# Eight slots for the exponentials, four products in one PSUM bank, and a key mask moved from TensorE to VectorE

## The chip, the core and the metric

One core of one Trainium2 chip runs the whole program. The metric is the device time of one execution in microseconds (us); a verdict compares medians of several runs. TensorE is called PE here, VectorE DVE, ScalarE ACT, GpSimd POOL, and SP is the engine that issues the DMAs.

## What is computed

The input x is 32 batches of 256 tokens with 256 features. Two attention blocks follow each other. Cut to what matters:

```python
# layer 0: linear attention, 8 heads of 32, softmax of k over the tokens
k = xn @ Wk + bk + (1.0 - src_mask) * -1000000.0
q = softmax(q.reshape(b, t, h, dh), axis=-1); k = softmax(k.reshape(b, t, h, dh), axis=1)
att = einsum('bnhd,bnhl->bhdl', k, v);  y = einsum('bnhd,bhdl->bnhl', q, att)
x = x + silu(_ln(y) * (1 + scale) + shift) @ W_out + b_out
# layer 1: full attention, 16 heads of 16, 256 x 256 scores
att = softmax(einsum('bnhl,bmhl->bnmh', q, k) + mask, axis=2)
y = einsum('bnmh,bmhl->bnhl', att, v)
x = x + silu(layer_norm(y) * (1 + scale) + shift) @ out_w + out_b
```

All masks of the inputs are ones; the kernel still applies them. Everything is float32.

## The kernel before

The work of a batch is cut into pieces, small functions that each run on one engine and end with an increment of a semaphore that bears the piece's name. PE has 18 kinds of piece for each batch, DVE, ACT and POOL have theirs. For each engine the pieces of all 32 batches stand in one hand-kept order (the long lists such as `rows(9, 0); rows(9, 1); pv(7, 0); ...` at the end of each engine's function), so that layer 0 of a batch runs beside layer 1 of an earlier one. An engine never goes round a piece that waits. Two tables at the top say which PSUM bank a piece writes (`BANK`) and which pieces must have ended before it may (`FREED`, waited for by `clear`, line 468). There are eight banks of 512 float32 per partition.

The pieces that the change and the prediction touch:

- `k0(b)` (PE, line 722): keys of layer 0, feature-major, 12 matmuls of 256 columns (line 733; weights and activations are each split into two f16 parts, three products), and after each half one more matmul (line 735) with a stationary operand `augs` of six rows that hold the bias in three bf16 parts and ones, against `augm`, whose rows 3 to 5 hold the mask in three bf16 parts. `am(b)` (SP, line 534) loads those rows, 1.5 KB a batch.
- `km(b)` (DVE, line 1215) takes the maximum over the tokens out of the PSUM bank of k0, `kn` (POOL) turns it into a bias, and `ke(b)` (ACT, line 1671) reads the same bank, takes the exponential with the scale in register `r_un`, and sums it. Then come `ktT` (transposes, line 718), `kt`, `att` (line 771) and `y0` (line 784).
- `rows(b, u)` and `cols(b, u)` (PE, lines 832 and 845), eight each a batch: the scores of layer 1, once for the maximum and once for the exponential. `max_` (DVE, line 1301) takes the maxima of rows, 128x1024 each. `exp(b, u)` (ACT, line 1783) writes 128x1024 exponentials of cols into one of five slots `PX`, chosen by `(8 * b + u) % 5`; it waits until `pv` of five units before has ended.
- `pv(b, u)` (PE, line 858): four matmuls of 256 columns in float32 (each stands twice in the trace), exponentials times values. The pairs u = 0,1 to 6,7 each write 256 columns of a bank of their own. `yt(b, g)` (ACT, line 1791), four a batch, copies each 128x256 to `YT`, and `ty` (PE, line 870) transposes that.
- Set-up: `row3` (PE, line 961) makes the bias of the keys as three equal rows with line 965 and 967; `p3` (DVE, line 1481) splits it into bf16 parts, `pa` (ACT) scales, `mb0` (DVE, line 1472) splits the mask in three, and the loads `mbd0`, `am` follow. `bb0`, `bb1`, `bb2` make three other biases (lines 976, 978), `fx0` (line 1002) the conditioning of layer 0.

In the written order of PE, `pv` and `att` stand in 140 unbroken stretches between pieces of other kinds, and pieces that use the full array (`k0`, `q0`, `v0`, `q1p`, `k1p`, `v1p`, `o0`, `o1`) are followed by another kind 177 times.

Of the kernel before, what the change touches and what calls it, by code (L numbers as in the profile page):

```python
# [13 lines left out]
P = 128  # L14
# [74 lines left out]
    "gy1T": "40666042444266640062604440660666",
    "go1": "23552057726271557471227354230111",  # L90
# [5 lines left out]
    "gpm": "-",  # L96
    "gt_w0": "hot",
    "ga_w0": "mx_w0",
    "gcnd": "-",
    "gbb1": "-",  # L100
    "grow3": "-",
    "gt_o0": "w0p",
    "gbb0": "-",
    "gfx0": "csT",
    "gq0": (
        "mx_o0 q1:1 mx_f0 perm qt:3 kt:5 Y0:5 at:7 qa:5 max:31 yt:11 yt:16 exp:41 exp:48 yt:28 yt:32 yt:35 Y0:16 "
        "max:102 at:19 st1:12 yt:54 yt:60 yt:64 st1:16 yt:71 yt:75 yt:79 Y0:27 max:190 exp:185 v:32 "),
    "gfm0": "mc",
    "gk0": (
        "fy0 bc0 at:2 mx_w1 bm Y0:4 max:2 exp:1 max:21 yt:8 yt:10 at:11 yt:19 yt:24 st1:6 vt:11 max:83 q1:18 Y0:17 "  # L110
        "yt:48 at:20 at:21 exp:120 yt:61 at:24 Y0:24 at:26 max:174 Y0:27 at:29 at:30 at:31 "),
    "gv0": (
        "bc1 p3 st0:1 w1p qt:3 kt:5 at:6 film1 exp:9 max:29 at:10 st0:9 yt:20 q1:14 x1:12 st1:7 st1:8 exp:84 Y0:17 "
        "max:110 st1:12 ka:18 st0:20 max:141 st1:16 st0:23 exp:153 max:174 yt:84 yt:88 exp:185 exp:191 "),
    "gt_f0": "f0m",
    "gkt": (
        "- qt:1 v:3+x1:1 bc2+at:3 v:4+ke:5 at:5+mx_f1 qt:6 yt:3+yt:2 max:25 q1:10+max:31 exp:26 exp:36 exp:45 qt:13 "
        "Y1:7 exp:68 max:91 qt:17 max:104 qt:19 exp:107 Y1:14 exp:125 exp:131 exp:137 exp:150 max:170 max:178 Y1:21 "
        "qt:29 Y1:23 exp:196 "),
    "gqt": (  # L120
        "kt:1 Y0:1 st0:2 Y0:3 qt:4 max:7 max:15 max:23 max:32 exp:27 Y1:4 max:57 Y1:6 max:72 exp:69 exp:73 Y1:10 "
        "exp:94 max:111 kt:21 max:128 Y1:15 max:144 exp:138 v:26+st0:23 exp:155 at:27+q1:28 exp:173 Y1:22 exp:187 "
        "st0:29 st1:24 "),
    "gat": (
        "q1:2 o0p kt:3 qa:1 vt:1 max:2 q1:7 kt:8 max:28 max:38 yt:15 yt:17 x1:10 Y0:13 max:75 exp:72 max:95 max:98 "
        "max:108 max:116 st1:13 st0:20 max:141 max:148 Y0:24 kt:26 yt:78 yt:83 yt:87 max:196 exp:191 Y0:31 "),
    "ga_o0": "ke:2",
    "gy0": (
        "ke:1+v:1 kt:2 kt:4 st0:3 kt:6 max:10 exp:7 max:27 max:36 exp:31 max:50 qt:12 max:68 max:74 max:84 exp:79 "
        "max:100 exp:95 max:115 exp:110 exp:119 max:138 exp:134 max:157 exp:149 exp:158 max:181 qt:28 exp:182 qt:30 "  # L130
        "max:211 max:218 "),
    "ga_f0": "v:2",
    "grw": "at:1",
    "gt_w1": "q1:3",
    "gy0T": (
        "qt:2 Y0:2 v:5+ka:1 max:3 Y0:6 Y0:7 yt:7+at:9 exp:24 exp:32 max:53 at:13+yt:23 yt:27+yt:26 max:76 max:85 "
        "exp:80 exp:87 Y0:18 max:117 Y0:20 Y0:21 st1:15 max:150 max:156 max:165 exp:160 exp:169 max:188 st1:22 "
        "max:203 max:213 max:220 max:229 "),
    "ga_w1": "film0",
    "gcol": "ke:3",  # L140
    "go0": (
        "st0:1 ke:4 qt:5 ke:7 q1:8 v:9 vt:5 ka:7 o:3 qa:9 v:14 exp:59 v:16 ka:13 ke:18 o:10 o:11 o:12 ke:22 ka:19 "
        "o:15 o:16 vt:21 o:18 yt:80 kt:29 exp:179 yt:93 exp:195 o:24 o:25 o:26 "),
    "gt_b": "q1:4",
    "ga_b": "mx_b",
    "gbb2": "kt:3",
    "gq1": (
        "fcs v:6 max:8 vt:3 exp:9 x1:7 o:2 ka:8 ke:13 x1:11 exp:59 x1:13 vt:12 exp:84 exp:90 exp:98 ka:17 x1:19 "
        "at:22 ka:20 ka:21 ka:22 exp:153 x1:25 ke:29 x1:27 o:22 ka:28 ka:29 vt:29 ka:31 o:27 "),
    "gfx1": "x1:2",  # L150
    "gk1": (
        "q1:5 q1:6 vt:2 ke:8 x1:6 o:1 v:11 v:12 v:13 o:5 qa:11 o:7 o:8 vt:13 max:102 v:20 v:21 o:13 v:23 vt:19 q1:25 "
        "ke:26 ke:27 o:19 q1:29 exp:179 q1:31 exp:195 yt:100 qa:30 vt:30 vt:31 "),
    "gfm1": "fy1",
    "gv1": (
        "at:4 Y0:5 ka:3 max:21 v:10 yt:12 max:46 max:56 st0:11 st1:6 exp:63 q1:17 yt:40 yt:45 max:110 yt:52 yt:55 "
        "qa:19 at:23 yt:68 o:17 yt:76 ka:24 max:183 max:190 yt:92 ke:32 at:32 st1:25 yt:107 max:237 yt:115 "),
    "gt_f1": "f1m",
    "gt_o1": "Y0:4",
    "gr0": (  # L160
        "ke:6+mx_o1 x1:4+v:7 exp:4 exp:11 exp:19 Y1:3 exp:35 vt:8+max:56 exp:53 kt:15 max:80 Y1:9 max:96 exp:91 "
        "max:112 exp:108 kt:22 exp:123 exp:132 max:152 exp:147 v:27+qa:23 exp:161 exp:171 o:21+q1:30 max:200 "
        "vt:27+o:23 exp:202 exp:212 exp:219 exp:227 exp:234 "),
    "gr1": (
        "x1:3+qt:5 o1p+qa:3 exp:6 qt:8 exp:21 max:41 exp:37 exp:44 kt:14 qt:14 kt:16 exp:76 exp:85 kt:19 exp:100 "
        "exp:109 exp:117 max:137 max:145 max:153 max:160 qt:26 max:177 max:185 kt:30 exp:188 max:209 exp:203 max:224 "
        "max:233 exp:228 exp:236 "),
    "gr2": (
        "max:1 max:9 v:8+ka:4 kt:9 max:33 max:42 max:49 kt:13 exp:52 exp:61 qt:15 max:90 kt:18 exp:93 max:114 qt:20 "
        "exp:118 exp:126 qt:23 exp:140 exp:148 max:169 Y1:20 max:186 exp:181 Y0:30 kt:32 exp:206 exp:214 exp:221 "  # L170
        "max:242 max:249 "),
    "gr3": (
        "ka:2+qa:2 kt:7 max:17 exp:13 max:35 yt:13+qa:7 exp:39 max:59 exp:54 yt:29+yt:30 max:82 exp:77 yt:41+qa:14 "
        "max:107 exp:101 max:123 qa:18+yt:57 Y0:22 max:146 exp:142 max:163 max:171 max:179 exp:175 max:194 exp:192 "
        "exp:199 exp:207 exp:215 exp:222 exp:229 exp:238 "),
    "gr4": (
        "max:4 max:11 max:20 exp:14 exp:23 max:44 Y0:11 exp:47 exp:56 at:15+yt:31 exp:70 max:92 exp:88 yt:47+yt:46 "
        "yt:50+yt:51 exp:112 yt:59+max:129 max:140 exp:135 max:155 exp:151 max:172 exp:167 exp:176 Y0:29 st1:23 "
        "exp:200 exp:208 max:227 exp:223 exp:230 max:251 "),
    "gr5": (  # L180
# [93 lines left out]
def bass_cond_seq(  # L274
# [7 lines left out]
    with ctx:  # L282
# [208 lines left out]
        def _(e):  # L491
# [55 lines left out]
            def split_in(b, i):  # L547
# [3 lines left out]
                if b < 3:  # L551

                    ready(e, *(("csT", "mc", "mb0", "mb1"), ("p3", "bc0", "bc1", "bc2", "fcs"), ("p3", "col"))[b])
# [140 lines left out]
        def _(e):  # L694
# [154 lines left out]
            def pv(b, u):  # L849
# [5 lines left out]
                if c == 0:  # L855
                    clear(e, f"gpv{g}", b)
# [1396 lines left out]
```

## Time and profile before

| | us |
|---|---|
| median of 3 runs | 807.55 (807.45 to 808.08) |
| the profiled execution | 807.33 |
| its span in the trace | 805.6 |
| mean granted clock of PE | 0.985 |

The profile is of one execution. Its times are us from the first instruction. An engine's busy time is the union of its instructions; matmuls are pipelined, so that a matmul of 0.27 us may start 0.11 us after the one before. The time that a piece holds PE is therefore read as the distance from its start to the start of the piece behind it.

### The profile page before, as it was taken

The numbers are of one execution on the slowest core, as the hardware profiler recorded it, in microseconds if no ns is written. First come the engines' busy times: TensorE is split into PE (matmuls) and PEld (weight loads), VectorE is DVE, ScalarE is ACT, GpSimd is POOL, SyncE is SP. The second block draws the span as 40 slices with busy tenths as digits, with TensorE's granted clock in tenths as the row PEclk, the third lists the DMA queues.
The fourth block names the chain that finished last, engine by engine and source line by source line (L and its number), as shares of the span: only waits on it lengthen the run. The fifth ranks groups of instructions, "written<-read, shape, count | busy, mean of one in ns | idle before, by whom it ended". The sixth has DMA issues, their size and how long they took to land. (4 is left out here: it accounts for less than half of the span.)

```text
span 805.6 us, 29123 instructions
## 1 busy us (share of the span) xinstructions
PE 772.6 (96%) x10431; PEld 538.0 (67%) x10431; DVE 710.9 (88%) x1392; ACT 701.6 (87%) x1658; POOL 681.8 (85%) x1085
## 2 busy tenths in 40 slices
PE   7999889999999999999999999999999999999985
PEld 3575765777777677777677767777677776656542
DVE  7698899999999899998899889999889989989953
ACT  2266768899999999999999999999999999999995
POOL 7379998989999999998899998998989988897334
PEclk8799999999999999999999999999999999999998
DMA  6423544444443544355653445444544363354301
GB/s 179 91 48 80 139 115 117 103 104 121 101 125 95 126 110 105 88 146 100 126 127 92 132 89 123 111 109 89 143 115 120 72 119 91 85 148 115 110 20 53
DMA packets 149283, 86.22 MB, mean 107 GB/s; under 512 B 87404, under 2 KB 141802, under 8 KB 149130
## 3 DMA queue, kind: packets, MB, share of 16 engines
q1 hardware_dynamic: 149140, 84.36, 43.1%
q8 instruction: 84, 1.38, 0.8%
q14 instruction: 59, 0.48, 0.2%
HBM read 39.64 MB, written 25.80 MB: 81 GB/s over the span
## 5 line engine op out<-in xcount | busy, mean ns | idle before, releaser
L1301 DVE TENSOR_REDUCE NM<-banks 128x4 f32<-128x1024 f32 x256 | 306.7, 1213 | 23.3 <-PE banks L832 21.0
L1783 ACT ACTIVATE wraw<-banks 128x1024 f32<-128x1024 f32 x154 | 157.2, 1038 | 8.5 <-PE banks L845 7.7
L1985 POOL TENSOR_TENSOR rs<-ve,nhalf 128x2 f32<-128x2 f32 x128 | 89.8, 703 | 32.9 <-ACT ve L1656 31.7
L1783 ACT ACTIVATE PX<-banks 128x1024 f32<-128x1024 f32 x102 | 104.0, 1034 | 5.5 <-PE banks L845 4.6
L832 PE MATMUL banks<-SK,SQ 51*128 51x256 f16 x1024 | 96.1, 272 | 3.6 <-DMA SK<-scr 1.2
L701 PE MATMUL banks<-wo,SH 128*128 128x256 f16 x768 | 95.5, 274 | 4.2 <-POOL SH L2073 4.2
L845 PE MATMUL banks<-SQ,SK 53*128 53x256 f16 x1024 | 96.8, 272 | 1.7 <-DVE NM L1301 1.1
L701 PE MATMUL banks<-wv,ZT 128*128 128x256 f16 x768 | 95.3, 275 | 0.9 <-DVE un L1436 0.8
L2073 POOL TENSOR_TENSOR SH<-ST,SH 128x512 f16<-128x512 f32 x64 | 74.5, 1166 | 23.7 <-ACT SH L1747 20.0
L858 PE MATMUL banks<-wraw,V 128*32 128x256 f32 x1232 | 87.7, 385 | 0.7 <-ACT PX L1783 0.3
L2010 POOL TENSOR_TENSOR ZHL<-Z,ZHL 128x256 f16<-128x256 f32 x128 | 83.1, 670 | 2.6
L701 PEld LDWEIGHTS banks<-wo,SH 128*128 128x128 f16 x768 | 71.7, 98 | 19.9 <-POOL SH L2073 5.8
L701 PEld LDWEIGHTS banks<-wv,ZT 128*128 128x128 f16 x768 | 72.2, 98 | 16.0 <-issue 6.7
L2101 POOL TENSOR_TENSOR AB<-R,AB 128x512 f16<-128x512 f32 x64 | 74.6, 1172 | 6.5 <-ACT AB L1763 6.3
L1734 ACT ACTIVATE TH<-banks,hB,hA 128x256 f32<-128x256 f32 x128 | 65.6, 569 | 10.4 <-PE banks L718 7.9
L1989 POOL TENSOR_SCALAR Z<-X,nm,rs 128x256 f32<-128x256 f32 x128 | 69.7, 553 | 4.5 <-issue 2.2
L1989 POOL TENSOR_SCALAR YN<-Y,nm,rs 128x256 f32<-128x256 f32 x128 | 69.7, 553 | 2.4
L1763 ACT ACTIVATE R<-banks,fcs 128x256 f32<-128x256 f32 x128 | 62.7, 490 | 9.7 <-PE banks L709 8.8
L832 PEld LDWEIGHTS banks<-SK,SQ 51*128 51x128 f16 x1024 | 38.7, 95 | 42.4 <-issue 21.9
L845 PEld LDWEIGHTS banks<-SQ,SK 53*128 53x128 f16 x1024 | 37.9, 96 | 43.4 <-issue 21.3
L1737 ACT ACTIVATE banks<-banks,fB,fA 128x256 f32<-128x256 f32 x128 | 64.2, 550 | 0.0
L1763 ACT ACTIVATE AB<-banks,fcs 128x256 f16<-128x256 f32 x128 | 63.2, 494 | 0.0
(187 smaller groups left out, 1782.8 us busy)
## 6 DMA issues: line engine op xcount, KB each, us to landing
scr<-AB SPq DMA_DIRECT2D x64, 256.0 KB, 2.6
X<-in_x_dram SPq DMA_DIRECT2D x32, 256.0 KB, 3.0
SQ<-scr SPq DMA_DIRECT2D x64, 128.0 KB, 2.8
SK<-scr SPq DMA_DIRECT2D x64, 128.0 KB, 2.9
out_dram<-wemb SPq DMA_DIRECT2D x32, 256.0 KB, 2.6
SQ<-scr SPq DMA_DIRECT2D x64, 64.0 KB, 2.8
SK<-scr SPq DMA_DIRECT2D x64, 64.0 KB, 3.0
wemb<-in_L_cond_W_emb_dram SPq DMA_DIRECT2D x1, 1024.0 KB, 5.3
```

Source lines behind the costliest of these rows:

```text
L701: m = PE.matmul(dst[:, t, :], zt[:, j, k, t * P:(t + 1) * P], w[:, i, k, :], start=(k, n) == (0, 0), stop=(k, n) == (1, 2))
L832: m = PE.matmul(banks[:, n + j % 2, (j // 2) * T:(j // 2) * T + T], SQ[p, r, h, c * P:(c + 1) * P], SK[p, r, h, :], start=True, stop=True)
L845: m = PE.matmul(banks[:, n + j % 2, (j // 2) * T:(j // 2) * T + T], SK[p, r, h, c * P:(c + 1) * P], SQ[p, r, h, :], start=True, stop=True)
L858: m = PE.matmul(banks[32 * j:32 * j + 32, n, 0:T], V1[:, r, c, 4 * g + j, :], px((8 * b + u) % 5)[:, at_px(j):at_px(j) + T], start=(c == 0 ...
L1301: V.tensor_reduce(NMe[:, c, :, 2 * g:2 * g + 2], banks[:, n:n + 2, :].rearrange("p a (h m) -> p a h m", m=T), AX.X, ALU.max, negate=True). ...
L1763: t = A.activation(dst, bank(home(f"g{c}1", b))[:, f, :], ACT.Identity, bias=fcs[:, i, f:f + 1], scale=(r_q, r_k)[i])
L1783: A.activation(px(v % 5), banks[:, n:n + 2, :].rearrange("p a n -> p (a n)"), ACT.Exp, scale=r_uu).then_inc(S["exp"])
L1985: G.tensor_tensor(rs[:, b % 2, l, :], ve[:, b % 2, l, :], nhalf[:, :], ALU.pow).then_inc(S[f"r{l}"])
L1989: i = G.tensor_scalar(dst[:, t], src[:, t], nm[:, b % 2, l, t:t + 1], rs[:, b % 2, l, t:t + 1], ALU.add, ALU.mult)
L2010: i = G.tensor_tensor(ZHL[:, l, b % 2, 1, k], z[:, :, k, :], ZHL[:, l, b % 2, 0, k], ALU.subtract)
L2073: G.tensor_tensor(by_half(SH[:, l, 1]), ST[:, l].rearrange("p h (q j) -> p h q j", j=HALF), by_half(SH[:, l, 0]), ALU.subtract).then_inc(S ...
L2101: G.tensor_tensor(AB[:, i, :, 1], R1[:, i], AB[:, i, :, 0], ALU.subtract).then_inc(S["sp" + c])
```

## The change

- `k0` loses its two extra matmuls. The mask is made as float32, scaled (`mbs`), written to DRAM, and `am(b)` loads it as a row of 256 spread over 128 partitions, 128 KB a batch, into three slots `MB`. `km(b)` becomes two `tensor_tensor_reduce` of 128x256 that multiply by the scale, add `MB`, write the result `KS` to SBUF, and take the maximum; `ke` reads `KS`. `row3`, `p3`, `pa`, `ru` go; `kb` makes the bias as a column per half, `kbc` copies it.
- `pv` writes all four pairs of a batch in two banks, four units to a bank; `yt` is two pieces of 128x512 instead of four of 128x256; `exp` has eight slots, three of them laid into weight buffers that are dead by then, and waits for the `pv` eight units before.
- All five orders and both tables are written anew. In the new order of PE `pv` and `att` stand in 117 stretches in place of 140, and full-array pieces are followed by another kind 170 times in place of 177.

```diff
             def k0(b):
                 e.wait_ge(d_z[0][b % 2], 16 * (b // 2 + 1))
-                e.wait_ge(d_am[b % 3], 16 * (b // 3 + 1))
...
-                    for k in range(2):
-                        for n, (i, j) in enumerate(PARTS):
-                            PE.matmul(dst[:, f, :], w[:, i, k, f * P:(f + 1) * P], zt[:, j, k, :],
-                                      start=(k, n) == (0, 0), stop=False)
-                    m = PE.matmul(dst[:, f, :], augs[:, f * P:(f + 1) * P], augm[:, b % 3, :], start=False, stop=True)
-                m.then_inc(S["k0"])
+                feat_major(bank(home("gk0", b)), ZT[:, b % 2, 0], W["k", 0]).then_inc(S["k0"])
...
             def pv(b, u):
                 g, c, r = u // 2, u % 2, b % 3
-                n = home(f"gpv{g}", b)
+                n, q = home(f"gpv{g // 2}", b), (g % 2) * T
...
-                if c == 0:
-                    clear(e, f"gpv{g}", b)
+                if u % 4 == 0:
+                    clear(e, f"gpv{g // 2}", b)
                 for j in range(4):
-                    m = PE.matmul(banks[32 * j:32 * j + 32, n, 0:T], V1[:, r, c, 4 * g + j, :],
-                                  px((8 * b + u) % 5)[:, at_px(j):at_px(j) + T], start=(c == 0), stop=(c == 1))
+                    m = PE.matmul(banks[32 * j:32 * j + 32, n, q:q + T], V1[:, r, c, 4 * g + j, :],
+                                  px(u)[:, at_px(j):at_px(j) + T], start=(c == 0), stop=(c == 1))
...
-            def row3():
+            def kb():
...
+                for f in range(2):
+                    h = slice(f * P, (f + 1) * P)
+                    for k in range(2):
+                        PE.matmul(at_kb(f), wraw[:, 1, k, h], lnc[:, 0, 1, k:k + 1], start=(k == 0), stop=False)
+                    t = PE.matmul(at_kb(f), brow[:, 3, h], one1[0:1, 0:1], start=False, stop=True)
...
             def km(b):
                 e.wait_ge(S["k0"], b + 1)
                 e.wait_ge(S["kn"], b)
-                V.tensor_reduce(kmr[:, :], bank(home("gk0", b)), AX.X, ALU.max, negate=True).then_inc(S["km"])
+                e.wait_ge(S["ke"], b)
+                e.wait_ge(d_am[b % 3], 16 * (b // 3 + 1))
+                for f in range(2):
+                    i = V.tensor_tensor_reduce(out=KS[:, f, :], in0=bank(home("gk0", b))[:, f, :], in1=MB[:, b % 3, :],
+                                               scale=un[:, 1:2], scalar=-3.0e38, op0=ALU.add, op1=ALU.max,
+                                               accum_out=kmr[:, f:f + 1])
...
             def am(b):
-                e.wait_ge(S["k0"], up(b - 2))
+                e.wait_ge(S["km"], up(b - 2))
                 e.wait_ge(l_mb, 16)
-                first(e, b, "cst")
-                e.dma_start(augm[3:6, b % 3, :], mbd[:, b, :]).then_inc(d_am[b % 3], 16)
+                e.dma_start(MB[:, b % 3, :], mbd[b].unsqueeze(0).to_broadcast([P, T])).then_inc(d_am[b % 3], 16)
...
-                    i = A.activation(KE[:, f, :], bank(home("gk0", b))[:, f, :], ACT.Exp, bias=kmx[:, f:f + 1],
-                                     scale=r_un, accum_out=ks[:, f:f + 1])
+                    i = A.activation(KE[:, f, :], KS[:, f, :], ACT.Exp, bias=kmx[:, f:f + 1], scale=1.0,
+                                     accum_out=ks[:, f:f + 1])
...
             def exp(b, u):
-                e.wait_ge(S["pv"], up(v - 4))
+                e.wait_ge(S["pv"], up(v - 7))
...
-                A.activation(px(v % 5), banks[:, n:n + 2, :].rearrange("p a n -> p (a n)"), ACT.Exp,
+                A.activation(px(u), banks[:, n:n + 2, :].rearrange("p a n -> p (a n)"), ACT.Exp,
                              scale=r_uu).then_inc(S["exp"])
 
             def yt(b, g):
-                e.wait_ge(S["pv"], 8 * b + 2 * g + 2)
+                e.wait_ge(S["pv"], 8 * b + 4 * g + 4)
...
-                A.activation(YT[:, g, :], banks[:, home(f"gpv{g}", b), 0:T], ACT.Identity).then_inc(S["yt"])
+                A.activation(YT[:, 2 * g:2 * g + 2, :].rearrange("p g t -> p (g t)"), banks[:, home(f"gpv{g}", b), :],
+                             ACT.Identity).then_inc(S["yt"])
```

## Rows read from the trace of the kernel before

**Rows 1.** The page, part 1: busy us of each engine, share, instructions
```profile
PE 772.6 (96%) x10431; PEld 538.0 (67%) x10431; DVE 710.9 (88%) x1392; ACT 701.6 (87%) x1658; POOL 681.8 (85%) x1085
```

**Rows 2.** Stretches: length, busy us (instructions) of PE, PEld, DVE, ACT, POOL, PE clock, DMA share, GB/s
```profile
200.00:700.00 500.00, 495.92 (x7094) 359.30 (x7094) 458.24 (x853) 474.10 (x1120) 456.15 (x719) 1.00 0.46 110
700.00:780.00 80.00, 75.81 (x1024) 43.85 (x1028) 68.24 (x100) 75.58 (x145) 50.51 (x83) 1.00 0.38 102
780.00:806.00 26.00, 15.27 (x208) 8.19 (x196) 8.78 (x19) 15.82 (x31) 8.21 (x10) 0.91 0.12 41
20.00:30.00 10.00, 10.00 (x18) 3.00 (x17) 5.66 (x16) 1.82 (x7) 5.82 (x12) 0.50 0.64 152
```

**Rows 3.** Waits, whole run: who for whom, us in total, times, longest
```profile
DVE NM L1301 <- PE banks L832: 21.0, 46, 1.1
```

**Rows 4.** Timeline of PE, 402 to 418 us: start, us, instructions
```profile
402.07 0.38 PE L845 MATMUL banks<-SQ,SK 53*128 53x256 f16 x4
402.38 1.48 PE L709 MATMUL banks<-ZT,wq 128*128 128x256 f16 x12
...
405.33 0.38 PE L832 MATMUL banks<-SK,SQ 51*128 51x256 f16 x4
405.56 0.38 PE L845 MATMUL banks<-SQ,SK 53*128 53x256 f16 x4
405.87 1.07 PE L858 MATMUL banks<-wraw,V 128*32 128x256 f32 x16
406.76 0.61 PE L858 MATMUL banks<-PX,V 128*32 128x256 f32 x8
407.30 0.61 PE L832 MATMUL banks<-SK,SQ 51*128 51x256 f16 x8
...
412.75 0.83 PE L733 MATMUL banks<-ZT,wk 128*128 128x256 f16 x6
...
414.38 0.39 PE L832 MATMUL banks<-SK,SQ 51*128 51x256 f16 x4
...
414.95 1.48 PE L701 MATMUL banks<-wv,ZT 128*128 128x256 f16 x12
416.27 1.47 PE L701 MATMUL banks<-wq,ZT 128*128 128x256 f16 x12
417.68 0.39 PE L845 MATMUL banks<-SQ,SK 53*128 53x256 f16 x4
```

**Rows 5.** Timeline of PE in the set-up, 18 to 57 us
```profile
18.63 1.87 PE L965 MATMUL banks<-wraw,lnc 128*3 128x256 f32 x4
...
21.37 0.37 PE L889 MATMUL banks<-ident,mxw 128*1 128x128 f32 x1
...
56.41 1.05 PE L1041 MATMUL banks<-one,SQ 1*128 1x1 f32 x8
```

**Rows 6.** Timeline of DVE in the set-up: the piece p3 starts
```profile
21.48 0.47 DVE L1484 TENSOR_SCALAR SQ<-banks,iu 3x256 f32<-3x256 f32 x1 [3.19 <-PE banks L967]
```

**Rows 7.** Groups of DVE instructions: count | busy us, mean ns | idle us before them
```profile
L1301 DVE TENSOR_REDUCE NM<-banks 128x4 f32<-128x1024 f32 x256 | 306.7, 1213 | 23.3 <-PE banks L832 21.0
L1196 DVE BATCH_NORM_AGGREGATE mv<-st 128x2 f32<-128x6 f32 x256 | 29.4, 158 | 0.7
L1271 DVE SCALAR_TENSOR_TENSOR ST<-TH,banks 128x512 f32<-128x512 f32 x64 | 43.0, 674 | 12.1 <-ACT banks L1737 11.8
L1218 DVE TENSOR_REDUCE kmr<-banks 128x2 f32<-128x512 f32 x32 | 21.6, 675 | 2.0 <-PE banks L735 1.8
```

**Rows 8.** Groups of ACT instructions, same columns
```profile
L1783 ACT ACTIVATE wraw<-banks 128x1024 f32<-128x1024 f32 x154 | 157.2, 1038 | 8.5 <-PE banks L845 7.7
L1791 ACT ACTIVATE wemb<-banks 128x256 f32<-128x256 f32 x128 | 49.1, 399 | 3.7 <-PE banks L858 3.1
L1678 ACT ACTIVATION_READ_ACCUMULATOR KE<-banks,km 128x1 f32 x64 | 13.9, 218 | 0.0
```

**Rows 9.** A DMA that spreads one row over 128 partitions: KB, us from issue to landing
```profile
bobc<-in_L_cond_b_out_dram SPq DMA_DIRECT2D x1, 128.0 KB, 3.8
```

More of the change, by code:

```diff
@@ new lines @@
+    "gat": "02103534430220202252152016454603",
+    "gy0": "40246604444640220044460260224620",
+    "ga_f0": "3",
+    "grw": "6",
+    "gy0T": "26420620400402466066624406026060",
+    "gt_w1": "6",
+    "gcol": "7",
+    "ga_w1": "6",
+    "go0": "73122522037741753263414555101252",
+    "gt_b": "2",
+    "ga_b": "2",
+    "gbb2": "0",
+    "gfx1": "6",
+    "gq1": "12252231366407423755054551103433",
+    "gfm1": "0",
+    "gk1": "13342321267506223745045440102452",
+    "gv1": "61245214202165521550504201135522",
@@ L91 @@
+    "go1": "43025651633254414144101344336666",
 }
@@ L475, in clear @@
                     ready(e, name)
-        at_row = lambda i: banks[:, home(f"grow{i}"), 0:D]
+        at_kb = lambda f, n=1: banks[:, home("gkb"), f:f + n]
         at_rows = lambda i: banks[0:1, home("grw"), i * D:(i + 1) * D]
@@ L648, in mbd0 @@
             def mbd0():
-                ready(e, "mb0")
-                e.dma_start(mbd.rearrange("c b t -> b c t"), mb3[:, :, :]).then_inc(l_mb, 16)
+                ready(e, "mbs")
+                e.dma_start(mbd, mbx).then_inc(l_mb, 16)
             def mbd1():
@@ new lines, in _ @@
+            y0T(15); k0(18); rows(12, 4); cols(10, 7); pv(10, 4); pv(10, 5); att(17); pv(10, 6); pv(10, 7)
+            rows(12, 5); y1T(9); cols(11, 0); q0(18); v0(18); rows(12, 6); rows(12, 7); cols(11, 1); k1p(14)
+            cols(11, 2); ty(10); o1(9); q1p(14); rows(13, 0); cols(11, 3); ktT(18); v1p(13); pv(11, 0); pv(11, 1)
+            cols(11, 4); cols(11, 5); rows(13, 1); o0(15); qtT(17); rows(13, 2); cols(11, 6); pv(11, 2); att(18)
+            pv(11, 3); cols(11, 7); rows(13, 3); y0(17); pv(11, 4); rows(13, 4); y0T(16); pv(11, 5); pv(11, 6)
@@ L1473, in mb0, with mbs @@
                 e.wait_ge(l_msk, 32)
[L1474 to L1489 removed]
+                V.tensor_scalar(mbf[:, 0, :], mrow[:, 0, :], -1.0, NEG, ALU.add, ALU.mult).then_inc(C["DVE"])
+            def mbs():
+                ready(e, "mb0", "w0p")
+                V.tensor_scalar(mbx, mbf[:, 0, :], iu[0:NB, 1:2], None, ALU.mult).then_inc(C["DVE"])
             def csl_():
@@ L1830, in csT_, with kbc @@
                              scale=0.5).then_inc(C["ACT"])
-            def pa():
-                ready(e, "w0p", "cst")
-                A.activation(augs[0:6, :], augs[0:6, :], ACT.Identity, scale=iu[0:6, 1:2]).then_inc(C["ACT"])
+            def kbc():
+                ready(e, "kb")
+                A.activation(bkc[:, :], at_kb(0, 2), ACT.Identity).then_inc(C["ACT"])
             def conds(l):
```

1183 lines of the change are left out of this document (562 added, 621 removed).

## The prediction

> **What bounds the kernel now.** I read the shares first. PE is busy 96% of the span, DVE, ACT and POOL 85 to 88% [rows 1]. An average hides stages, so next come the stretches: from 200 to 700 us PE is busy 495.9 of 500 us at the full clock (granted share 1.00), while DVE has 458.2, ACT 474.1 and POOL 456.2 [rows 2]. To see what one batch costs I count records. The pieces of a batch make 322 on PE (12 for each of seven projections, 14 for k0, 8 for each of four half transposes, 32 att, 16 y0, 32 rows, 32 cols, 64 pv, 16 ty). The 7094 records of the stretch are 22.0 batches, so a batch takes 22.7 us. Of these PE is busy 22.5, ACT 21.6, DVE 20.8, POOL 20.7. DVE waits for a maximum because PE has not written the scores, 46 times, 21.0 us in all [rows 3]: PE sets the pace and the others wait for it. From 780 us on, the last 26 us, PE is busy 15.3 and ACT 15.8, neither full: there the chain through the last batches counts [rows 2]. So what leaves PE before 780 us leaves the time, nearly one for one, as long as no other engine takes over, and what leaves ACT is worth little but in the tail.
>
> **How a piece is priced.** Busy times of matmuls overlap, so a piece is priced by the distance to the next start. A four-matmul piece of scores behind its like takes 0.23 us (405.33 to 405.56); in front of pv it takes 0.31 (405.56 to 405.87) [rows 4]. Two pv in a row take 0.89, 0.445 each (405.87 to 406.76), the last one in front of rows 0.54 (406.76 to 407.30) [rows 4]. A projection takes 1.32 in front of another (414.95 to 416.27) and 1.41 in front of cols (416.27 to 417.68) [rows 4]; cols take 0.31 in front of one (402.07 to 402.38) [rows 4]. Changing the way in which the array is cut costs 0.08 to 0.10 us at each change.
>
> **The change, part by part.**
>
> *Two matmuls less in k0.* k0 in front of rows takes 1.63 us (412.75 to 414.38), a projection of 12 matmuls in front of cols 1.41 [rows 4]. The difference is 0.22 us, 32 times: 7.0 us off PE, all of it before 780 us. Ends: 6.4 (two matmuls at 0.10) to 7.5.
>
> *Fewer changes of kind.* PE's new order has 117 stretches of pv and att in place of 140. Each stretch less saves an entry (0.31 - 0.23 = 0.08) and an exit (0.54 - 0.445 = 0.10): 23 x 0.18 = 4.1 us. Full-array pieces are followed by another kind 7 times less, at 0.08 for the entry and 0.09 for the exit: 1.2 us. Together 5.3 us. Eight slots are what allows this: exp may run eight units ahead of pv, not five, so PE can find several units ready. Ends: 0, if PE then waits inside the longer stretches for exp (1.04 us each, more than twice a pv [rows 8]), to 6.
>
> *Set-up on PE.* row3 holds PE from 18.63 to 21.37, 2.7 us, and at half clock: PE is busy 10.0 of 10 us there at a granted share of 0.50, the lower level of 1.2 GHz [rows 5, 2]. In its place comes kb, four matmuls with a column as the moving operand and two with one row. Nearest below, four one-row matmuls of one column, eight records, take 1.05 us [rows 5]; nearest above is row3 itself. I take 1.2 us for kb, near the former, because a moving operand of one column is what they share: 1.5 us less. p3 goes from DVE: it stood waiting 3.2 us for row3 [rows 6], in front of the low parts of the weights; that wait vanishes, and late next is then PE's own set-up, which has no gap there. Ends for the set-up: 0 to -4 us, the latter if the earlier weights also fill gaps of PE in the first 140 us.
>
> *km on DVE.* One reduction of 128x512 (0.675 us) becomes two fused ones of 128x256 with a second operand. The nearest row with a second operand is L1271, 0.674 us for 512 columns; 256 columns less at the slope between 1024 and 512 columns ((1.213 - 0.675) / 512 = 1.05 ns a column) leave 0.405 each, 0.81 for both: +0.14 us a batch [rows 7]. Ends: -0.1 (no dearer than a reduction, ends overlapping) to +2.1 (each as dear as the reduction of 1024 columns, plus an instruction of 0.158 to read the sum out: 2 x 1.213 + 2 x 0.158 = 2.74). At +0.14, DVE goes from 20.8 to 21.0 us of a batch that now lasts 22.3. It is covered by 1.9 us of idle time of DVE a batch; if that is gone, each 0.1 us costs 3 us in the run. km now also waits for the ke before and for the DMA of the mask. Behind km in DVE's queue stand maxima and statistics; ke of the batch before is a batch (22 us) old, except in the first batches, where km(1) now stands behind ke(0).
>
> The Trainium skill ("VectorE: DVE Perf Modes", section "Two Vector instructions with no wait between them") speaks against this part: an op that also writes out its accumulator is two instructions, the main one and a read of the accumulator. The trace agrees for ACT alone, where each sum is followed by a read of 218 ns [rows 8]; DVE has no such op here. By that rule km costs 2 x 0.405 + 2 x 0.158 = 1.13 us, +0.45 a batch, and the sum below would end some 1 us later.
>
> *ACT.* Four yt of 0.399 us cost 49.1 / 128 = 0.384 each in union; 256 more columns cost (1.038 - 0.399) / 768 x 256 = 0.21 [rows 8]. Two of 0.60 for four of 0.384: 0.34 us less a batch. ke reads SBUF, taken as equal. ACT is not the limit before 780 us, so I count nothing; in the tail it may give 0.3 us.
>
> *DMA.* am grows from 1.5 to 128 KB a batch, with the same number of issues on SP. A load of that form takes 3.8 us to land among the first loads [rows 9]; it may start two batches ahead. The engines of the DMA are busy 46% and move 110 GB/s [rows 2], 2.5 MB a batch of 22.7 us; 0.13 MB more adds 5% of that, two points. Counted at nothing, covered by two batches of 22 us. mbs, mbd0 and am(0) now follow the weight scale; they end well before km(0) needs them if PE's set-up is the pace. Ends: 0 to +1.5.
>
> *Given back.* A shorter pace leaves DVE, ACT and POOL less slack (1.4, 1.1 and 1.6 us a batch), and PE's waits grow. PE's own idle time is 4.1 us in 500 [rows 2]; I add half of that over the run, 2 us. Ends: -2 (slots and banks come free earlier) to +8.
>
> **Sum.** -7.0 - 5.3 - 1.5 + 2 = -11.8 us. Against the profiled execution's 807.33 that is 795.5; it stands 0.2 below the median, which I neglect.
>
> **The rivals.**
>
> *Another engine takes over part of the pace.* DVE at +0.45 a batch or ACT, whose 1.1 us of slack is the least, hands over late so often that the gain from order is lost. For: on average all four engines are within 9% of each other. Against: DVE idles 42 of 500 us [rows 2]. Then only the 7.0 stays, less 1 us: 801.
>
> *More than I sum.* DVE and POOL start earlier, PE's waits in the first 140 us and the chain of the tail shrink, with eight slots and k0's bank free at km, not at ke. For: set-up had a wait of 3.2 us on DVE alone [rows 6]. Against: PE has no gap where p3 stood. 5 to 7 us more: 789.
>
> *Slower: km saturates DVE.* Place: km in DVE's queue, ahead of maxima that feed the chain to exp. It decides from +1.9 us a batch, the idle time of DVE. At the upper end, 2.74 us, DVE needs 20.8 + 2.07 = 22.9 us a batch; with 0.8 us of idle time left that is 23.7 in place of 22.7, in some 29 batches: 836. Against: it needs a price three times that of the nearest row.
>
> *Not faster.* The new order brings waits that eat all: 807. What the change says it does, it does: records of line 735 must vanish, so that form of this rival has no chance.
>
> **How the numbers follow.** A measurement of this kernel can tell some 0.2% (1.6 us) from no change. The forecast, 791 to 799, has 0.60; another engine taking over, 799 to 805, 0.18; more than summed, 786 to 791, 0.13; not faster 0.04; slower 0.05. Faster: 0.60 + 0.18 + 0.13 = 0.91. The range is 788 to 803: it takes in the ends of order and give-back, and leaves out the last two rivals and the outer parts of the others.
>
> **What would show it.** Records of PE fall by 64 and a few of set-up; k0 in front of rows takes 1.41 us; pv stretches are longer at 0.445 a unit; a batch in the middle takes 22.3 us with PE busy over 98%. km shows as two instructions of about 0.4 us (two more of 0.16 if the sum is read out apart), yt as 64 of 0.6 us. The first projection starts 1 to 2 us earlier. The forecast is wrong if PE's busy share between 200 and 700 us falls below 97% with waits for exp or for DVE; if km takes over 2.6 us; or if the tail after the last maximum grows by more than 2 us.

## The result, and the profile after

| | before | changed |
|---|---|---|
| median, range of the runs, us | 807.82 (807.45 to 808.51), 4 runs | 798.0 (792.64 to 805.6), 4 runs |
| granted clock of PE in these runs | 0.985 (profiled) | 0.987, 0.987, 0.979, 0.977 |
| the profiled execution, its span | 807.33, 805.6 | 794.21, 792.4 |

The ratio is 0.985 (0.980 to 0.990): 1.5% less time, with an interval clear of 1, as forecast, and inside the range of 788 to 803. A ratio leaves out runs that lie over 1.5% above the fastest of their kernel, so it can stand a little off the ratio of the medians; one run of the kernel before at 1242.26 us, with a granted clock of 0.612, is left out of every figure below. What no step had foreseen is the spread: the changed kernel's runs differ by 13 us where those of before differed by 1. The faster runs are those with the higher granted clock. Two executions are therefore compared below in a second way, **at full clock**: the time less the span x (1 - mean granted clock). That treats the time at half clock (1.2 GHz) as if all of it went at half speed, which is an approximation. A straight line through the 11 runs of `again` (below) gives 6.8 us for each 0.01 of clock, where this measure takes off 8.0, so between kernels whose clocks differ by 0.007 it can be wrong by some 1 us. For the four runs it gives 782.4 to 787.1, median 784.4.

Busy time, share and instructions of each engine, which answer to [rows 1]:

```profile
PE 759.8 (96%) x10373; PEld 540.0 (68%) x10373; DVE 714.3 (90%) x1478; ACT 697.4 (88%) x1594; POOL 682.1 (86%) x1111
```

PE has 58 records less: 64 of line 735 gone, 6 more in the set-up. It is 12.8 us less busy, and the span is 13.2 us shorter. DVE is 3.4 us busier. The stretches, which answer to [rows 2]:

```profile
200.00:700.00 500.00, 496.05 (x7184) 364.91 (x7176) 469.31 (x933) 479.72 (x1096) 464.81 (x749) 1.00 0.50 119
700.00:780.00 80.00, 74.59 (x1014) 42.00 (x1011) 61.70 (x95) 75.21 (x130) 41.37 (x71) 0.99 0.31 86
```

A batch now has 320 records on PE, so 7184 are 22.45 batches, 22.27 us each (22.7 before; forecast 22.3). Of these PE is busy 22.1, ACT 21.4, DVE 20.9, POOL 20.7. PE's own idle time is 32.6 us in the whole span, 33.0 before (35.9 in the second execution profiled, `again`): nothing clear was won or lost.

Where the time went is seen best between two fixed points of the work, the starts of the 64th and of the 240th of the 256 maxima (L1301, then L1294). That is 22 batches of maxima, at a granted clock of 1.00 throughout. Before, the changed kernel, and the changed kernel in `again`:

```profile
262.38:742.70 480.32, 475.10 (x6723) 338.52 (x6720) 438.12 (x802) 454.96 (x1063) 432.74 (x683) 1.00 0.47 111
```

```profile
259.25:729.59 470.34, 467.07 (x6694) 338.99 (x6689) 440.69 (x856) 451.89 (x1020) 433.74 (x699) 1.00 0.49 118
```

```profile
267.06:739.53 472.47, 467.57 (x6694) 338.77 (x6689) 440.56 (x856) 451.90 (x1020) 433.73 (x699) 1.00 0.50 117
```

This stretch is 7.8 to 10.0 us shorter, so most of the gain is made in the middle. The work in it is nearly the same: 29 instructions of PE fewer, where 44 left with `k0`. The two executions of one kernel differ by 2.1 us in it, and that is what a single trace can tell.

What the first batches show is the set-up of PE, which answers to [rows 5]:

```profile
13.40 0.61 PE L952 MATMUL banks<-lnc,wraw 128*128 128x1 f32 x4
13.94 0.39 PE L953 MATMUL banks<-one,SK 1*128 1x1 f32 x2
14.25 1.01 PE L952 MATMUL banks<-lnc,wraw 128*128 128x1 f32 x4
15.19 0.58 PE L953 MATMUL banks<-one,SK 1*128 1x1 f32 x2
...
19.58 6.00 PE L989 MATMUL banks<-wemb,csT 128*32 128x512 f32 x8
...
27.42 1.48 PE L703 MATMUL banks<-ZT,wk 128*128 128x256 f16 x12
28.74 1.47 PE L695 MATMUL banks<-wq,ZT 128*128 128x256 f16 x12
```

`kb` holds PE from 13.40 to some 15.8 us, 2.4 us, at two levels of the clock (its second half takes 1.01 for what the first does in 0.61). The first projection starts at 27.42; before it was 30.84. But these 3.4 us are clock. Up to the first projection, before and after:

```profile
0.00:30.84 30.84, 25.96 (x68) 9.79 (x69) 20.48 (x50) 6.85 (x19) 21.23 (x44) 0.72 0.62 164
```

```profile
0.00:27.42 27.42, 24.54 (x80) 11.78 (x81) 18.37 (x45) 6.78 (x19) 16.94 (x35) 0.81 0.71 185
```

At full clock that is 0.72 x 30.84 = 22.2 us and 0.81 x 27.42 = 22.2 us: the set-up of PE is no shorter. In `again` the first projection starts at 30.35, at a granted share of 0.78. And the groups of DVE, which answer to [rows 7]:

```profile
L1294 DVE TENSOR_REDUCE NM<-banks 128x4 f32<-128x1024 f32 x256 | 307.3, 1213 | 16.9 <-PE banks L817 15.0
...
L1208 DVE CUSTOM_DVE_ANT_0 KS<-banks,MB,un 128x256 f32<-128x256 f32 x64 | 28.1, 476 | 1.4 <-PE banks L703 1.2
...
L1208 DVE DVE_READ_ACCUMULATOR2_ANT kmr<- 128x1 f32 x64 | 5.3, 83 | 0.0
```

`km` is two pairs of a fused reduction of 476 ns and a read of its accumulator of 83 ns: (28.1 + 5.3) / 32 = 1.04 us a batch, where one reduction took 0.675. The maxima L1294 still wait for PE, 15.0 us (21.0 before [rows 3]). On ACT, `yt` is 64 of 610 ns (this answers to the second of [rows 8]):

```profile
L1770 ACT ACTIVATE wemb<-banks 128x512 f32<-128x512 f32 x64 | 38.9, 610 | 1.8 <-PE banks L843 0.8
```

Prices of pieces, from the timeline of PE, which answer to [rows 4]:

```profile
406.13 1.09 PE L843 MATMUL banks<-wemb,V 128*32 128x256 f32 x16
407.00 0.66 PE L843 MATMUL banks<-worw,V 128*32 128x256 f32 x8
407.59 0.39 PE L817 MATMUL banks<-SK,SQ 51*128 51x256 f16 x4
...
417.68 1.48 PE L703 MATMUL banks<-ZT,wk 128*128 128x256 f16 x12
419.09 0.39 PE L830 MATMUL banks<-SQ,SK 53*128 53x256 f16 x4
```

Two `pv` take 0.87, the last one 0.59 (0.54 before), and a 12-matmul L703 piece, the form that `k0` now has, 1.41. So the pieces cost about what was forecast.

### The profile page after: what moved, and what is told of

Read it like the earlier page. It is cut to its first block and busy times, and to the rows that moved or that the text cites. A ratio compares the mean times of both kernels' runs of the same rounds, so it can differ in the third digit from the quotient of the medians.

```text
span 792.4 us, 28934 instructions
## 1 busy us (share of the span) xinstructions
PE 759.8 (96%) x10373; PEld 540.0 (68%) x10373; DVE 714.3 (90%) x1478; ACT 697.4 (88%) x1594; POOL 682.1 (86%) x1111
## 5 line engine op out<-in xcount | busy, mean ns | idle before, releaser
L1294 DVE TENSOR_REDUCE NM<-banks 128x4 f32<-128x1024 f32 x256 | 307.3, 1213 | 16.9 <-PE banks L817 15.0
L1762 ACT ACTIVATE wraw<-banks 128x1024 f32<-128x1024 f32 x96 | 96.9, 1032 | 5.2 <-PE banks L830 4.6
L830 PE MATMUL banks<-SQ,SK 53*128 53x256 f16 x1024 | 95.1, 271 | 3.1 <-DVE NM L1294 1.2
L703 PE MATMUL banks<-ZT,wk 128*128 128x256 f16 x768 | 94.8, 273 | 1.5 <-DMA ZT<-ZHL 1.1
L703 PEld LDWEIGHTS banks<-ZT,wk 128*128 128x128 f16 x768 | 71.0, 98 | 16.5 <-issue 4.8
L1709 ACT ACTIVATE TH<-banks,hB,hA 128x256 f32<-128x256 f32 x128 | 65.7, 570 | 13.8 <-PE banks L712 11.8
L817 PEld LDWEIGHTS banks<-SK,SQ 51*128 51x128 f16 x1024 | 37.1, 95 | 51.2 <-issue 25.0
L1762 ACT ACTIVATE wemb<-banks 128x1024 f32<-128x1024 f32 x64 | 65.9, 1042 | 3.0 <-PE banks L830 2.6
L1762 ACT ACTIVATE PX<-banks 128x1024 f32<-128x1024 f32 x64 | 64.6, 1037 | 1.0 <-PE banks L830 0.5
L830 PEld LDWEIGHTS banks<-SQ,SK 53*128 53x128 f16 x1024 | 40.2, 96 | 36.3 <-issue 18.3
```

The costliest lines, as they stand in the source:

```text
L703: m = PE.matmul(dst[:, f, :], w[:, i, k, f * P:(f + 1) * P], zt[:, j, k, :], start=(k, n) == (0, 0), stop=(k, n) == (1, 2))
L817: m = PE.matmul(banks[:, n + j % 2, (j // 2) * T:(j // 2) * T + T], SQ[p, r, h, c * P:(c + 1) * P], SK[p, r, h, :], start=True, stop=True)
L830: m = PE.matmul(banks[:, n + j % 2, (j // 2) * T:(j // 2) * T + T], SK[p, r, h, c * P:(c + 1) * P], SQ[p, r, h, :], start=True, stop=True)
L1294: V.tensor_reduce(NMe[:, c, :, 2 * g:2 * g + 2], banks[:, n:n + 2, :].rearrange("p a (h m) -> p a h m", m=T), AX.X, ALU.max, negate=True). ...
L1709: A.activation(TH[:, l, :, k, :], fresh(n, k), ACT.Tanh, bias=hB[:, l, k, b:b + 1], scale=hA[:, l, k, b:b + 1])
L1762: A.activation(px(u), banks[:, n:n + 2, :].rearrange("p a n -> p (a n)"), ACT.Exp, scale=r_uu).then_inc(S["exp"])
```

## The experiments

In all of them the kernel before ran on the same chip: 27 runs with a median of 808.26 us beside the first four kernels, 31 with 808.9 beside the next four, 9 with 809.2 beside `before_km_more`, `km_in_one` and `mask_small`, 17 with 809.75 beside the last. At full clock it is 795.2, 795.7, 795.4 and 795.4, so that measure can be compared across chips. Its runs beside the first four lie between 805.56 and 811.78 us, with granted clocks from 0.977 to 0.987. No kernel tried here that leaves nothing out has a lower time at full clock than the changed kernel. The medians at full clock carry an uncertainty (95%) of 1.0 to 1.6 us in each difference, 2.0 for `six_slots`, estimated from the spread of the runs.

The stretch between the 64th and the 240th maximum, at a granted clock of 1.00, one execution each, read in the same way as above:

| kernel | us | against |
|---|---|---|
| `before_less_rows` | 476.8 | before, 480.3 |
| `before_km_more` | 484.1 | before, 480.3 |
| `after_with_rows` | 473.9 | changed, 470.3 and 472.5 |
| `six_slots` | 471.6 | changed |
| `km_more` | 481.4 | changed |
| `yt_in_four` | 471.5 | changed |
| `mask_small` | 473.2 | changed |
| `km_one_bf16` | 472.7 | changed |

**`again`: the changed kernel once more, no edit.**

> The changed kernel once more, to see why its first four runs lie from 792.6 to 805.6 us. Theory A (the granted clock of TensorE): the long runs have more time at the lower level, so their mean granted clock is below 0.98 and the time follows it, about 1 us more for each 2 us at 1.2 GHz; the short ones, at 0.987, lie within 2 us of 793.5. Rival (waits): the runs spread at an equal clock. A expects a correlation of time with clock: near 793 at 0.987, 800 to 806 at 0.977 to 0.979.

Measured: 802.59 us (797.59 to 808.84, 11 runs), ratio 0.992 (0.989 to 0.995). The granted clock went from 0.985 in the fastest to 0.968 in the slowest run. At full clock all but one lie between 783.0 and 785.7, median 784.3. So the spread is the granted clock, and the work itself is 795.2 - 784.3 = 10.9 us shorter. Not all of that reaches the time that counts: the median clock is 0.977 here and 0.984 in the runs of before beside it, and the medians in us are only 5.7 apart (808.26 and 802.59). Where it comes in is seen in one stretch of two executions, columns as in [rows 2]. The changed kernel as first profiled (794.21 us):

```profile
45.00:55.00 10.00, 9.95 (x97) 8.26 (x97) 8.82 (x33) 5.26 (x16) 8.32 (x15) 1.00 0.11 22
```

The same kernel in `again` (805.24 us):

```profile
45.00:55.00 10.00, 10.00 (x41) 3.98 (x41) 5.42 (x23) 3.88 (x13) 6.49 (x12) 0.50 0.28 49
```

PE is busy throughout in both, but does 41 matmuls in place of 97: half clock. The timelines of PE in the set-up, first of the changed kernel, then of `again`:

```profile
42.63 1.02 PE L1019 MATMUL banks<-wraw,lnc 128*1 128x256 f32 x4
43.59 0.59 PE L1020 MATMUL banks<-SK,one 1*1 1x256 f32 x2
...
45.58 1.48 PE L703 MATMUL banks<-ZT,wk 128*128 128x256 f16 x12
```

```profile
45.37 1.86 PE L1019 MATMUL banks<-wraw,lnc 128*1 128x256 f32 x4
47.16 1.01 PE L1020 MATMUL banks<-SK,one 1*1 1x256 f32 x2
```

`again` reaches this place 2.7 us late, and then pays 1.86 where the other pays 1.02. Both executions had a first stretch at half clock from about 14 us and another near 100 us. In `again` the first one lasted longer (a granted share of 0.67 from 24 to 30 us, against 0.97), which is why it comes late, and the stretch shown here came on top.

**`before_less_rows`: one part alone, in the old order.** The kernel before without the matmuls of line 735. It leaves out the bias and the mask of layer 0's keys.

```diff
-                    m = PE.matmul(dst[:, f, :], augs[:, f * P:(f + 1) * P], augm[:, b % 3, :], start=False, stop=True)
```

> The kernel before without its two extra matmuls in k0, everything else as before (left out: bias and mask of the keys of layer 0). Theory 1 (TensorE sets the pace, a piece costs its distance to the next start): 32 x 0.22 us less, 807.8 - 7.0 = 800.8. Rival 2 (another engine takes over): less than 4 us, over 804. The clock in the middle stays at the full level.

Measured: 807.39 us (802.21 to 810.05, 12 runs), ratio 0.999 (0.997 to 1.000). At full clock 791.1 (788.1 to 793.0): 4.1 us less than before, not 7.0, and so between the two theories. In the middle stretch it is 3.5 us for 22 x 0.22 = 4.8. In measured time hardly anything is left, because the granted clock fell with it, from a median of 0.984 to 0.980.

**`after_with_rows`: the same part put back in the new order**, as two matmuls of zeros per `k0`.

```diff
+                    m = PE.matmul(dst[:, f, :], zers[:, f * P:(f + 1) * P], zerm[:, :], start=False, stop=True)
```

> The changed kernel with two matmuls of zeros of the same form put back in each k0, in the new order. Theory 1: 7.0 us more than the changed kernel at an equal clock, 800.5 where that has 793.5. Rival 2: TensorE has idle time to hide them, under 4 us more.

Measured: 804.44 us (800.27 to 808.72, 12 runs), ratio 0.995 (0.993 to 0.998). At full clock 790.0, that is 5.7 above `again`; in the middle stretch 1.4 to 3.6 more. The 64 matmuls, priced at 7.0 us of PE, are thus worth 4.1 in the old order and 5.7 in the new one: 0.6 to 0.8 of their price.

**`six_slots`: the extra slots taken away.** An `exp` waits for the `pv` six units before it.

```diff
-                e.wait_ge(S["pv"], up(v - 7))
+                e.wait_ge(S["pv"], up(v - 5))
```

> The changed kernel with exp waiting for the pv six units before, in place of eight; nothing else. Theory 1 (the longer stretches of pv rest on units that ran ahead): TensorE waits for exp in some batches, 1 to 6 us more. Rival (the order is what counts and the planner kept exp no more than six ahead): within 0.5 us of the changed kernel at an equal clock.

Measured: 801.35 us (795.57 to 807.56, 6 runs), ratio 0.988 (0.985 to 0.992). At full clock 784.5, against 784.3 with eight. The seventh and eighth slot are worth nothing that six runs can tell (2 us either way), and the middle stretch is no longer. What the sixth is worth wasn't tried.

**`km_more` and `before_km_more`: one more reduction in `km`**, once in each order.

```diff
+                V.tensor_reduce(kxx[:, :], bank(home("gk0", b)), AX.X, ALU.max)
```

> The changed kernel with the old reduction of 128x512 (0.675 us) done in km as well as the new work: 32 x 0.6 = 19 us more on VectorE in the run. Theory 1 (TensorE sets the pace, VectorE has about 1.4 us of slack a batch): at most 3 us more than the changed kernel at an equal granted clock. Rival 2 (VectorE is at its limit after the change): 8 to 19 us more.

> The kernel before with a second reduction of 128x512 in km, the same 32 x 0.6 = 19 us more on VectorE as in the run of the changed kernel that came out some 15 us longer. Times at the full clock (time less the part of the span that the mean granted clock is short of 1) are 795 for the kernel before. Theory 3 (all engines hand over in order and VectorE was already nearly as much of a limit before): 10 to 16 us more here too. Rival 2 (VectorE took over only with the change, in which km grew by 0.4 us a batch while TensorE shrank): at most 6 us more here.

The stretch from 200 to 700 us, of `km_more` and then of `before_km_more`:

```profile
200.00:700.00 500.00, 488.31 (x7014) 356.79 (x7014) 470.46 (x935) 470.64 (x1072) 455.96 (x735) 1.00 0.49 115
```

```profile
200.00:700.00 500.00, 493.79 (x7020) 355.47 (x7019) 463.68 (x865) 470.23 (x1112) 450.85 (x714) 1.00 0.46 109
```

Measured: `km_more` 813.25 us (811.37 to 816.53, 10 runs), ratio 1.006 (1.004 to 1.009), at full clock 800.0. `before_km_more` 822.09 us (817.37 to 823.62, 5 runs), ratio 1.016 (1.013 to 1.018), at full clock 806.5. DVE's busy time rose by 18.9 us (against `again`) and 18.2 us (against before), the time at full clock by 15.7 and 11.1: 0.8 and 0.6 us for each us of DVE work. DVE was idle for 30 and 36 us of these 500, and PE, with 11.7 and 6.2 us idle, more than without the reduction (3.9 and 4.1). DVE has no free slack in either order, though its share was 88%. But the two orders lose it in different places. In the middle stretch, where DVE's busy time rose by 9.2 us before and by some 10.5 us after, the old order lost 3.8 us and the new one 9 to 11: 0.4 against 0.8 to 1.1 us for each us of DVE work. The rest of the old order's loss, 6 us, comes ahead of the 64th maximum (268.67 us against 262.38, at a granted share of 0.96 in both). So in the middle DVE was a weak limit before, and with the change it became no weaker a one than PE.

**`yt_in_four`: four copies of 128x256 again**, two in a row in each `yt`.

```diff
+                for i in range(2):
+                    m = A.activation(YT[:, 2 * g + i, :], banks[:, home(f"gpv{g}", b), i * T:(i + 1) * T], ACT.Identity)
```

> The changed kernel with each yt of 128x512 made by two instructions of 128x256: 32 x 2 more instructions, about 5 to 11 us more on ScalarE. Theory 1: hidden but for the tail, 0 to 1.5 us more at an equal clock. Rival (ScalarE had taken over part of the pace, so the saving on it carried the gain): 5 us or more.

```profile
L1771 ACT ACTIVATE wemb<-banks 128x256 f32<-128x256 f32 x128 | 42.6, 398 | 1.8 <-PE banks L843 1.1
```

Measured: 805.6 us (799.61 to 810.42, 10 runs), ratio 0.995 (0.992 to 0.998); at full clock 788.35, 4.1 more than `again`, for 3.7 us more of ACT's busy time (42.6 against 38.9). That is between the theory (0 to 1.5) and the rival (5 or more). Where it is lost isn't shown: the middle stretch took 471.5 us, no more than in the two executions of the changed kernel. So ACT isn't free in the total, but that it holds up the pace is not shown.

**`mask_small`: the load of the mask made small**, 1 KB into one partition. It leaves the mask out on 127 of 128 partitions.

```diff
+                e.dma_start(MB[0:1, b % 3, :], mbd[b].unsqueeze(0).to_broadcast([1, T])).then_inc(d_am[b % 3], 16)
```

> The changed kernel with am loading 1 KB a batch in place of 128 KB (the mask of ones only; a mask that masks would reach one partition only). Theory as predicted (the DMA is covered): within 1 us of the changed kernel at the full clock, 784. Rival (the larger loads delay X, scr or the transposes): 2 to 5 us less.

Measured: 796.18 us (794.51 to 800.15, 5 runs), ratio 0.984 (0.981 to 0.987), at full clock 781.8 (779.9 to 783.8). The 128 KB a batch cost some 2.5 us at full clock, with an uncertainty of 1.6 us, and the profiled execution shows nothing of it in the middle stretch (473.2 us). This is the lowest median of all, but it isn't a kernel to keep.

**`km_in_one` and `km_one_bf16`: one fused reduction of 128x512 in `km`**, with the mask loaded twice (256 KB a batch), and then the same with the mask in bf16 (128 KB).

```diff
+                e.dma_start(MB[:, b % 3, :].rearrange("p (f t) -> p f t", f=2),
+                            mbd[b].unsqueeze(0).unsqueeze(0).to_broadcast([P, 2, T])).then_inc(d_am[b % 3], 16)
...
+                V.tensor_tensor_reduce(out=KS[:, :, :].rearrange("p f t -> p (f t)"), in0=banks[:, home("gk0", b), :],
+                                       in1=MB[:, b % 3, :], scale=un[:, 1:2], scalar=-3.0e38, op0=ALU.add, op1=ALU.max,
+                                       accum_out=kmr[:, 0:1]).then_inc(S["km"])
```

> The changed kernel with km as one fused instruction of 128x512 (one maximum for both halves of the features, which the softmax allows; the mask is loaded 512 wide, 256 KB a batch) in place of two of 128x256: about 0.3 us a batch less on VectorE, 9 us in the run. Theory 3 and rival 2: each us of VectorE is worth 0.8 us, so 6 to 8 us less than the changed kernel at the full clock (784), near 777. Theory 1 (TensorE alone sets the pace): within 1.5 us of it.

> The changed kernel with km as one fused instruction of 128x512, as in the run that loaded 256 KB of mask a batch, but with the mask as bf16, so that am again loads 128 KB in rows of 1 KB. Theory 3 with the DMA as the cause of that run's loss: VectorE 0.22 us a batch less, 7 us in the run, each worth 0.8: about 5.5 us less than the changed kernel at the full clock, 779, and the granted clock back at 0.975 to 0.987; median near 796. Rival (the one-instruction form itself delays kn and ke and so the chain of layer 0): no less than the changed kernel at the full clock, 784 or more.

Measured: `km_in_one` 828.75 us (827.43 to 830.05, 5 runs), ratio 1.024 (1.022 to 1.026), at full clock 801.1. Its group of DVE, the load of the mask (KB, us from issue to landing) and two of PE's waits:

```profile
L1208 DVE CUSTOM_DVE_ANT_0 KS<-banks,MB,un 128x512 f32<-128x512 f32 x32 | 23.7, 741 | 13.1 <-PE banks L704 10.7 <-DMA MB<-mbd 2.1
```

```profile
MB<-mbd SPq DMA_DIRECT2D x32, 256.0 KB, 5.6
```

```profile
PE banks L818 <- DMA SQ<-scr: 6.4, 6, 1.8
...
PE banks L704 <- DMA ZT<-ZHL: 5.0, 3, 3.8
```

The operation came out as meant (23.7 + 2.6 us of DVE in place of 28.1 + 5.3), and the kernel is 17 us slower at full clock: the load takes 5.6 us, and PE now waits for other loads. `km_one_bf16` settles which: the same operation with 128 KB gives 804.26 us (798.11 to 811.07, 12 runs), ratio 0.993 (0.991 to 0.996), at full clock 787.1. So 14 of the 17 us are the second 128 KB, or the twice as many packets of the f32 form (256 a batch in place of 128), which no run tells apart. The other loads land only a little later (`X` 3.6 us against 3.2, `SK` from `scr` 3.2 against 3.1). The other 3, slower with 7 us less of DVE work, stay open: the group of DVE shows more waiting for PE in front of it,

```profile
L1207 DVE CUSTOM_DVE_ANT_0 KS<-banks,MB,un 128x512 f32<-128x512 f32 x32 | 23.7, 740 | 6.6 <-PE banks L703 6.0 <-DMA MB<-mbd 0.3
```

but one execution can't tell what of it is cause. The sensitivity of DVE is thus measured for work added, not for work taken away. The first expectation (6 to 8 us less) missed, and of the second the rival held.

**`warm_setup` and `warm_waits`: can the clock be held up?** 8 filler matmuls of 128x512 in the set-up's early pieces, or 27 ahead of eleven pieces of the first batches that PE had waited for (the expectation says 25; the trace has 27).

```diff
+            def warm(n, count):
+                for i in range(count):
+                    PE.matmul(banks[:, n, :], wz[:, 0:P], wz[:, :], start=True, stop=True)
```

> The changed kernel with 8 filler matmuls (128x512 f16) between the float32 matmuls of the set-up, in banks that nobody uses yet. Theory A (the granted clock makes the spread): the stretch at half clock after 14 us is gone or shorter, each us of it less gives back about half a us: 2 to 4 us less than the changed kernel, and a higher mean clock. Rival: the fall at 14 us does not depend on this work; the fillers cost 2 to 3 us.

> The changed kernel with 25 filler matmuls (128x512 f16, 5.3 us at full clock) in front of eleven pieces in the first 125 us at which TensorE stood waiting. Theory A: the stretches at half clock near 45 to 55 us and near 100 us go, the runs lie close together, at 0.984 to 0.99, near the fast end of the changed kernel (792 to 798) or 2 us above it. Rival: the spread stays and the median grows by the fillers.

Measured: 807.14 us (800.21 to 812.35, 10 runs), ratio 0.996 (0.992 to 1.000), and 806.75 us (803.45 to 814.91, 10 runs), ratio 0.999 (0.996 to 1.003). At full clock 790.7 and 789.8: the fillers cost 5 to 6 us, and the granted clock still went from 0.972 to 0.989 and from 0.966 to 0.985. Both missed.

## Why the prediction was right, and which of its steps were wrong

The total held: 10.9 us less at full clock, and 798.0 measured, for a forecast of 11.8 less and 795.5. In part that is luck, twice over. The terms have errors that cancel: the two matmuls and the set-up gave less than forecast, `km` and the load cost what was counted at little or nothing, and the new order gave more. And the first four runs were kind: over the 11 runs of `again` the median is 802.59, just inside the range, with five runs above 803.

*Two matmuls less in k0.* Right as a price of PE (a 12-matmul piece takes 1.41 us, where `k0` in front of rows took 1.63), wrong as a price of time: 4.1 us in the old order, 5.7 in the new one.

*"What leaves PE ... leaves the time, nearly one for one".* This step failed in part. PE was busy 99% of the middle, yet the matmuls taken from it gave 0.6 of their price, and 18 us added to DVE cost 11 already in the kernel before, 6 of them before the middle. A reading that fits, though no run isolates it: each engine works off a fixed order, so a piece that gets longer delays its reader now and then even where the average share says there is room. The first rival, that another engine takes over part of the pace, is in this sense partly true, and more so with the change: in the middle a microsecond on DVE costs 0.4 before and 0.8 to 1.1 after. But its outcome (that only the 7.0 stays) didn't come, as the other parts gave as much again.

*Order, set-up and yt.* From 791.1 (`before_less_rows`) to 784.3 it is 6.8 us, where the forecast had 5.3 + 1.5. It is net of what `km` and the load cost, so together they gave more. No run has one of them alone, but the traces part them. The set-up's 1.5 isn't there: `kb` costs 2.4 us and not 1.2 (its price at half clock was mis-sized), and the first projection, though 3.4 us earlier, comes at the same 22.2 us of full clock. In the middle the changed kernel is 4.3 to 6.5 us shorter than `before_less_rows` (476.8 against 472.5 and 470.3), where the forecast's 5.3 for the order comes to 3.6 for 22 of 32 batches, and undoing `yt` changes nothing there that a trace can tell. So the order gave this, and gave at least what was forecast; that it did so by fewer changes of kind on PE is argued, not shown. "Eight slots are what allows this" is wrong as it stands: six give the same.

*ACT counted at nothing.* Wrong in the total: undoing `yt` costs 4.1 us, though none of it shows in the middle. The saving in busy time was 49.1 - 38.9 = 10.2 us, as priced (0.34 x 32 = 10.9). `ke` isn't equal: 509 ns reading SBUF, against 485 reading PSUM, 1.5 us in the run, of which the shorter read of its sum (200 ns against 218) gives 1.1 back.

*km on DVE.* Mis-sized: +0.37 us a batch (1.04 against 0.675), forecast +0.14. The Trainium skill's rule ("VectorE: DVE Perf Modes", section "Two Vector instructions with no wait between them"), by which an op that writes its accumulator is two instructions, is what the trace shows; the estimate by it was 1.13 us, near the measured 1.04, since the read takes 83 ns and not 158. The 0.23 us that were missed make 7.4 us of DVE in the run, and by the measured 0.8 that would be some 6 us of time, an estimate only: `km_one_bf16` shows that taking such work away doesn't simply give it back. That slack covers such an addition is refuted by `km_more`; what `km`'s own growth cost, no run shows.

*DMA counted at nothing.* 2.5 us at full clock, above the upper end of 1.5 given, but by no more than the uncertainty. The share rose by four points (0.46 to 0.50, at a shorter batch), not two, and the engines of the DMA are still half idle: the share doesn't explain the price. Beside it the change made `kn` on POOL two operations of 196 and 195 ns in place of one of 262, which no step had.

*Given back.* The prediction added 2 us; the unpriced costs of km and DMA stand in its place. PE's waits did not grow in the first profile (32.6 us against 33.0) and grew by 2.9 in `again`.

*The range and the clock.* No term held the granted clock, so the range was right for a reason that it did not have: the runs from 792.6 to 808.8 differ by it, and three of the first four lie in the range. With the change the median clock fell from 0.984 to 0.977, and that takes back 5 of the 10.9 us in the medians.

## What to carry to other kernels

Where several engines in fixed orders are each busy 88% or more, price work on any of them at a measured share of its duration (here 0.6 to 0.8 us per us added to PE or DVE over the whole run), found by adding a known operation, and not by whether it is the busiest. Measure the price again after the change, and by stage: on DVE it went from 0.4 to 0.8 or more in the middle. Compare executions at equal granted clock before an effect of 1% is believed or denied: a saving of 4 us on PE came out as 0.9 in the medians, with a clock that stood 0.004 lower. Then look at the plain medians again, for a lower clock that comes with a change is a part of what it costs. A fused reduction has a second instruction that reads its result, and a load that spreads rows over 128 partitions can cost time even when it is issued two batches early: with 256 KB a batch PE waited for other loads.

## What the runs showed of the hardware that was not expected

The granted clock of one kernel on one chip varies from run to run: 0.968 to 0.985 in `again`, which is 11 us. It is made up of a few stretches at 1.2 GHz in the first 115 us, in which PE stays busy and does half as much, and of shorter ones in the last 25. The latter cost little: from the 240th maximum to the end the changed kernel took 62.8 us at a granted share of 0.97 and 63.9 us at 0.91, 1.1 us for what the measure at full clock counts as 3 to 4. Which stretches fall varies too. The rows of `again`, around 100 us:

```profile
95.00:103.00 8.00, 5.34 (x90) 4.06 (x92) 7.75 (x17) 6.96 (x23) 7.61 (x11) 1.00 0.43 104
103.00:112.00 9.00, 8.39 (x71) 6.57 (x72) 7.59 (x13) 2.88 (x7) 8.30 (x14) 0.62 0.62 148
```

PE was busy only 5.34 of 8 us there and then fell to 0.62 for the next 9. Ahead of the fall at 45 us it had waited too (0.84 us for V in the faster execution, 1.41 in `again`). Waits go before both, but the fillers, which were put in front of such waits, did not keep the clock up, so what decides it in a given run is left open. `km_in_one`, in which PE waited for loads in the middle too, had the lowest clock of all, 0.965 to 0.967 in each of its 5 runs.
